# Two-layer graph convolution: 39 groups of three blocks by one-hot products and 30 blocks by gathered rows, in place of 38 and 33

## The chip, the cores and the metric

The kernel runs on one core of one Trainium2 chip, in one launch. The metric is the device time of that core in microseconds. Engine names are those of the profile: PE is TensorE's matmul stream and PEld its weight loads, DVE is VectorE, ACT is ScalarE, POOL is GpSimd, SP is SyncE, which here only issues DMAs.

## The reference, cut to what matters

```python
NTOKEN, NINP, NHID, NEDGE = 18750, 64, 128, 300000
def gcn_conv(x, W, b, src, dst, n):
    h = x @ W
    deg = jnp.zeros((n,), h.dtype).at[dst].add(1.0) + 1.0
    dinv = jax.lax.rsqrt(deg)
    norm = dinv[src] * dinv[dst]
    agg = jax.ops.segment_sum(h[src] * norm[:, None], dst, num_segments=n)
    return agg + h * (dinv * dinv)[:, None] + b
h = gcn_conv(emb, W1, b1, src, dst, NTOKEN)
nodes = gcn_conv(h, W2, b2, src, dst, NTOKEN)
return nodes[input.reshape(-1)].reshape(b_, l_, NINP)   # input: 512 x 200
```

The costly part is the sum over 300,000 edges into 18,750 nodes, done twice, once in each layer.

## The kernel before

The nodes are 147 blocks of 128 (`BLOCKS`). A node's row is 64 numbers held as three bf16 parts (`ROW` = 192 columns), and the table of all rows lies in SBUF (`xtab`) and in DRAM (`table`, for layer 1 `table1`).

**Before the layers** (to about 1075 us) the degrees are counted, the edges are sorted by a bitonic sort on DVE and PE, and the node rows are weighed. After it the sorted keys lie in DRAM and are read back by cell.

**Two ways of summing the edges of a destination block.** The destination blocks are split by the constant `SPE`:

- The first `SPE * SUP` blocks (38 groups of `SUP` = 3) are summed by one-hot products. A group has `CELLS` = 49 cells, one for every window of `WIN` = 3 source blocks. So there are `ST` = 49 * `SPE` cells, worked in batches of `BT` = 4: `NB` = 466 batches a layer. For a cell PE multiplies three one-hot matrices with three blocks of `xtab` (L989, "gather"), ACT copies the result to SBUF as `grow` (L830), and PE multiplies it by three one-hot matrices of the destinations (L1054, "scatter") into the group's sums. DVE makes both one-hots: `dwin` (L1560), one instruction for each cell, and `s_oh` (L1465), three instructions for each pair of batches. A batch therefore has 12 gather and 12 scatter matmuls of 192 columns.
- The other `ZB` = 33 blocks are summed by items "z": POOL gathers 128 rows from DRAM by one indirect DMA (L684) into one of `RING` = 18 places of `zring`, DVE makes one one-hot `zoh` (L1544), PE makes one matmul (L1020). A block has `ZT` = 18 such items, the last one 10. What did not fit into a cell goes the same way: `OT` = 3 * `SPE` items "o" (in layer 0, for its first groups, "m"), each with one gather, one one-hot `ooh` (L1547) and three matmuls (L1025; L1037 to L1043 for "m").

So a layer has 586 + 114 = 700 items. `planned` puts them into the batches by hand: each batch j is filled up to `total * (j + 1) // NB` items, o items go to the last three batches of their group, and the first item of a new z block waits until three batches after the last item of the block before:

```python
goal = total * (j + 1) // NB if j < NB - 4 else total
while left and given + len(now) < goal and (left[0][2] or j >= wait_until):
    ...
    if n == (ZT if blk < ZB - 1 else ZLAST) - 1:
        wait_until = j + 3
```

In layer 1 `wait_until` begins at 10. The order on PE is written out: in batch j it waits for DVE's `d_ready`, does the items of the batch, and then for each half the gather of batch j + 1 and the scatter of batch j, waiting for ACT's copy. DVE works one batch ahead and waits for `ymm` (the scatter of the batch before last); POOL waits for `zmm`, by which PE gives a place of the ring back. SP broadcasts the source numbers of two batches (`keys<-srel`, 256 KB) and stores finished groups. When a group closes, DVE takes its sums out (L1471), and when a z block closes, with L1477.

**After the layers** the requested rows are picked and written by indirect DMAs (L730, L739); that part has no `SPE` in it.

Of the kernel before, what the change touches and what calls it, by code (L numbers as in the profile page):

```python
# [52 lines left out]

SUP, SPE, WIN = 3, 38, 3
CELLS = BLOCKS // WIN
ST = SPE * CELLS
ZB0 = SPE * SUP
# [1658 lines left out]
```

## Time and profile before

| what | value |
|---|---|
| time, median of 3 runs | 4097.41 us (4090.86 to 4101.44) |
| time of the profiled execution | 4114.96 us |
| its span, first to last instruction | 4113.1 us |
| layer 0, layer 1 | 1357 us, 1288 us |
| PE, DVE, POOL busy over the span | 68%, 73%, 45% |
| mean granted TensorE clock | 0.848 |

Busy time is a share of the span; a granted clock of 1.0 is 2.4 GHz, 0.5 is 1.2 GHz. A matmul's duration in the trace covers its way through the array, and matmuls overlap; their pace is read from the starts. The wait named behind an idle time is the one that ended it; "remote" and "issue" are ends that the trace ties to no instruction.

### The profile page before, as it was taken

The page shows a single profiled execution, that of the slowest core. Times are in us where ns is not written, and L with a number is a line of the kernel's source. Part 1 is how long each engine was busy: PE and PEld are TensorE (multiplying, and loading weights), DVE is VectorE, ACT ScalarE, POOL GpSimd, SP SyncE. Part 2 cuts the span into 40 slices and gives each one's busy share as a digit, 9 for nine tenths or more (in the row PEclk, how much of TensorE's full clock was granted, in tenths as well). Part 3 has the DMA queues.
Part 4 walks back from the last instruction along what each step waited for, and adds up shares of the span by engine and source line. Part 5 has one row for each costly group of instructions (what it writes and reads, how often), then busy time and mean ns, then how long its engine had stood idle before and what let it go on. Part 6 is the DMA issues. An engine that isn't in the chain of part 4 may idle for free.

```text
span 4113.1 us, 74778 instructions
## 1 busy us (share of the span) xinstructions
PE 2787.5 (68%) x27730; PEld 2494.4 (61%) x27730; DVE 3019.4 (73%) x8656; ACT 1326.7 (32%) x3124; POOL 1867.6 (45%) x1717
## 2 busy tenths in 40 slices
PE   6996434421477888888888867888888888883000
PEld 5884222211367777877877766888887888882000
DVE  9999999999577887877777866777777777773000
ACT  5774212210433333433333322333333333331000
POOL 2000000000465556666656645666666565555765
PEclk9997566655699999999999988999999999996555
DMA  3000000000223233333333342333333333336400
GB/s 75 0 0 4 19 12 16 19 4 0 64 77 83 76 78 79 86 79 79 81 81 82 83 134 69 80 84 82 85 82 81 77 82 80 78 81 252 60 24 9
DMA packets 202648, 269.00 MB, mean 65 GB/s; under 512 B 99119, under 2 KB 111704, under 8 KB 202039
## 3 DMA queue, kind: packets, MB, share of 16 engines
q1 hardware_dynamic: 147912, 185.41, 15.1%
q0 software_dynamic: 54416, 79.31, 10.3%
q8 instruction: 203, 3.33, 0.3%
q14 instruction: 117, 0.96, 0.1%
HBM read 213.38 MB, written 52.14 MB: 65 GB/s over the span
## 4 chain that ended last, share of the span: by engine, by line
PE 47%; DVE 32%; issue 6%; another core or an unknown queue 6%; POOL 5%; ACT 2%; POOLq 1%; SPq 1%; DMA 0%; DVEq 0%; ACTq 0%
PE ps L989 17%; PE ps L1054 17%; PE ps L871 8%; DVE oh L1560 7%; DVE keys L1287 6%; DVE keys L1288 6%; DVE keys L1465 4%; POOL arena L730 3%; PE ps L1020 2%; POOL out L739 2%; DVE zoh L1544 2%; PE ps L937 1%; PE ps L1025 1%; POOLq L739 1%
## 5 line engine op out<-in xcount | busy, mean ns | idle before, releaser
L684 POOL DMA_INDIRECT zring<-table,sidx x1400 | 1560.2, 1114 | 1055.2 <-PE ps L1020 533.8
L989 PE MATMUL ps<-arena,keys 128*128 128x192 bf16 x11184 | 1283.9, 253 | 271.1 <-issue 132.1
L830 ACT ACTIVATE steps_oh<-ps 128x384 bf16<-128x384 f32 x1864 | 898.7, 490 | 1723.7 <-PE ps L989 1296.2
L1054 PE MATMUL ps<-steps_oh,oh 128*128 128x192 bf16 x11172 | 1276.9, 252 | 1.9 <-issue 1.9
L989 PEld LDWEIGHTS ps<-arena,keys 128*128 128x128 bf16 x11184 | 970.5, 100 | 340.1 <-issue 205.2
L1054 PEld LDWEIGHTS ps<-steps_oh,oh 128*128 128x128 bf16 x11172 | 985.7, 100 | 12.8 <-issue 3.1
L1560 DVE TENSOR_SCALAR oh<-io_h,dl 128x384 bf16<-128x384 int16 x3724 | 960.0, 319 | 44.9 <-remote 28.0
L1465 DVE TENSOR_SCALAR keys<-keys,lanes 128x1024 bf16<-128x1024 int16 x1398 | 596.5, 480 | 16.7 <-DMA keys<-srel 10.6
L639 POOL DMA_INDIRECT arena<-line,row_i x16 | 15.8, 988 | 1030.4 <-DVEq L1351 1025.9
L1544 DVE TENSOR_SCALAR zoh<-io_h,dl 128x128 bf16<-128x128 int16 x1172 | 261.2, 263 | 301.6 <-remote 147.5
L937 PE MATMUL ps<-ident,keys 128*128 128x128 f32 x464 | 100.1, 409 | 319.8 <-DVE keys L1288 315.3
L1020 PE MATMUL ps<-zring,zoh 128*128 128x192 bf16 x1172 | 217.7, 253 | 119.3 <-DVE oh L1560 79.7
L937 PEld LDWEIGHTS ps<-ident,keys 128*128 128x128 f32 x464 | 92.5, 222 | 335.6 <-DVE keys L1288 330.7
L1287 DVE TENSOR_TENSOR keys<-keys 128x1280 f32<-128x1280 f32 (+4 forms) x233 | 278.9, 1197 | 17.6 <-ACT keys L801 9.5
L1288 DVE TENSOR_TENSOR keys<-keys 128x1280 f32<-128x1280 f32 (+4 forms) x233 | 277.4, 1190 | 0.0
L758 ACT ACTIVATE steps_oh<-colf,arena 128x128 bf16<-128x128 f32 x784 | 240.4, 389 | 78.8 <-PE ps L871 78.7
L1138 DVE TENSOR_TENSOR oh<-iorep,arena 128x1024 bf16<-128x1024 bf16 (+1 forms) x392 | 258.6, 714 | 0.4 <-DVE arena L1188 0.4
L871 PE MATMUL ps<-oh 128*128 128x147 bf16 x1568 | 231.1, 314 | 0.3 <-DVE oh L1138 0.3
L1020 PEld LDWEIGHTS ps<-zring,zoh 128*128 128x128 bf16 x1172 | 99.2, 99 | 173.5 <-DVE oh L1560 119.2
L871 PEld LDWEIGHTS ps<-oh 128*128 128x128 bf16 x1568 | 173.2, 118 | 40.7 <-DVE oh L1138 17.6
L1547 DVE TENSOR_SCALAR ooh<-io_h,dl 128x384 bf16<-128x384 int16 x228 | 71.6, 324 | 161.2 <-PE ps L1054 89.6
L739 POOL DMA_INDIRECT out<-arena,oidx x130 | 127.7, 982 | 67.9 <-issue 67.9
(249 smaller groups left out, 1615.8 us busy)
## 6 DMA issues: line engine op xcount, KB each, us to landing
keys<-srel SPq DMA_DIRECT2D x466, 256.0 KB
out<-zring SPq DMA_DIRECT2D x1, 25600.0 KB
zring<-table,sidx POOLq DMA_INDIRECT x1400
table<-arena SPq DMA_DIRECT2D x19, 384.0 KB, 2.8
table<-sgn_l SPq DMA_DIRECT2D x38, 144.0 KB
nodes<-arena SPq DMA_DIRECT2D x38, 96.0 KB
arena<-in_L_rec_edge_index SPq DMA_DIRECT2D x2, 1171.5 KB, 6.6
arena<-nodes,oidx POOLq DMA_INDIRECT x130
```

Of the source, the lines that this page charges most:

```text
L684: pool.indirect_dma_start(out=zring[:, i % RING, :], out_offset=None, in_=rows_of, in_offset=bass.IndirectOffsetOnAxis(ap=sidx[:, col:col ...
L830: act.activation(grow[:, j % 2, h * 2 * ROW:(h + 1) * 2 * ROW], pg[h][:, 0:2 * ROW], ACT.Copy).then_inc(evac, 1)
L871: mm = pe.matmul(bank[:, 0:BLOCKS], lane[:, t // TT, :, t % TT] if steps is None else stp[:, t, :], blk[:, t // TT, :, t % TT], start=Fals ...
L989: mm = pe.matmul(pg[t // 2][:, t % 2 * ROW:(t % 2 + 1) * ROW], s_oh[:, j // 2 % 2, k, e:e + P], xtab[:, (w * WIN + k) * ROW:(w * WIN + k + ...
L1020: pe.matmul(pz[:, 0:ROW], zoh[:, u, :], zring[:, u, :], start=False, stop=(n == (ZT if blk < ZB - 1 else ZLAST) - 1)).then_inc(zmm, 1)
L1054: mm = pe.matmul(sums(sl, k), dwin[:, j % 2, t, k * P:(k + 1) * P], grow[:, j % 2, t * ROW:(t + 1) * ROW], start=False, stop=(w == CELLS - ...
L1138: dve.tensor_tensor(o.rearrange("p (s j t) -> p s j t", s=HH // TT, t=TT), iorep[:, 0:m, :].unsqueeze(1).to_broadcast([P, HH // TT, m, TT] ...
L1287: dve.tensor_tensor(b[:, :, 0, :], a[:, :, 0, :], a[:, :, 1, :], ALU.min).then_inc(k_stage, 1)
L1288: dve.tensor_tensor(b[:, :, 1, :], a[:, :, 0, :], a[:, :, 1, :], ALU.max).then_inc(k_stage, 1)
L1465: made = dve.tensor_scalar(s_oh[:, p % 2, k, :], srow[:, p % 2, :], lanes[:, k:k + 1], None, ALU.is_equal)
L1544: dve.tensor_scalar(zoh[:, place[item], :], io_h[:, 0:P], dl[:, col:col + 1], None, ALU.is_equal)
L1560: made = dve.tensor_scalar(dwin[:, j % 2, t, :], io_h[:, off:off + SUP * P], dl[:, c:c + 1], None, ALU.is_equal)
```

## The change

One constant:

```diff
-SUP, SPE, WIN = 3, 38, 3
+SUP, SPE, WIN = 3, 39, 3
 CELLS = BLOCKS // WIN
 ST = SPE * CELLS
 ZB0 = SPE * SUP
```

What follows from it by the kernel's own formulas, for each layer: `ST` 1862 becomes 1911, `NB` 466 becomes 478, `NPAIR` 233 becomes 239, `ZB` 33 becomes 30 (with `ZB0` 114 becoming 117), z items 586 become 532, `OT` 114 becomes 117, all items 700 become 649. `GT`, the number of cell tables of 128 cells, stays 15. `planned` spreads 649 items over 478 batches (1.36 a batch) where it spread 700 over 466 (1.50).

## Rows read from the trace of the kernel before

**Rows 1.** The page: span, engines, TensorE's clock in 40 slices.

```profile
span 4113.1 us, 74778 instructions
...
PE 2787.5 (68%) x27730; PEld 2494.4 (61%) x27730; DVE 3019.4 (73%) x8656; ACT 1326.7 (32%) x3124; POOL 1867.6 (45%) x1717
...
PEclk9997566655699999999999988999999999996555
```

**Rows 2.** Windows, both layers: length, busy PE, PEld, DVE, ACT, POOL, clock, DMA.

```profile
1075.00:2432.00 1357.00, 1117.86 (x12248) 1032.14 (x12246) 1045.33 (x3906) 490.36 (x1067) 813.02 (x725) 0.95 0.32 79
2448.00:3736.00 1288.00, 1104.05 (x12212) 1033.65 (x12210) 935.94 (x3505) 449.48 (x933) 763.69 (x692) 0.95 0.33 82
```

**Rows 3.** Timeline, PE, around a stop in layer 1 (start, us, idle before).

```profile
2982.14 0.66 PE L989 MATMUL ps<-arena,keys 128*128 128x192 bf16 x6
2982.63 0.66 PE L1054 MATMUL ps<-steps_oh,oh 128*128 128x192 bf16 x6
...
2984.57 0.66 PE L1054 MATMUL ps<-steps_oh,oh 128*128 128x192 bf16 x6
2988.26 1.14 PE L989 MATMUL ps<-arena,keys 128*128 128x192 bf16 x6 [3.03 <-issue]
```

**Rows 4.** The chain that ended last, both layers, by line.

```profile
by line: PE ps L989 26.0%; PE ps L1054 25.9%; DVE oh L1560 11.3%; another core or an unknown queue 8.7%; DVE keys L1465 5.4%; issue 5.0%; PE ps L1020 3.3%; DVE zoh L1544 3.3%; PE ps L1025 1.7%; ACT steps_oh L830 1.5%; DVE arena L1471 1.4%; 
```

**Rows 5.** Groups by line, both layers (busy us, mean ns, idle before, releasers).

```profile
L684 POOL DMA_INDIRECT zring<-table,sidx x1397 | 1557.1, 1115 | 1040.9 <-PE ps L1020 533.8 <-issue 287.6 <-remote 107.2
L989 PE MATMUL ps<-arena,keys 128*128 128x192 bf16 x11167 | 1281.0, 253 | 261.4 <-issue 132.1 <-ACT steps_oh L830 94.9 <-DMA arena<-table 17.7
...
L1560 DVE TENSOR_SCALAR oh<-io_h,dl 128x384 bf16<-128x384 int16 x3718 | 958.5, 319 | 44.9 <-remote 28.0 <-PE ps L1054 14.9 <-issue 1.1
...
L1544 DVE TENSOR_SCALAR zoh<-io_h,dl 128x128 bf16<-128x128 int16 x1169 | 260.6, 263 | 301.6 <-remote 147.5 <-PE ps L1054 146.5 <-issue 4.3
...
L1547 DVE TENSOR_SCALAR ooh<-io_h,dl 128x384 bf16<-128x384 int16 x228 | 71.6, 324 | 161.2 <-PE ps L1054 89.6 <-remote 66.9 <-issue 3.3
```

**Rows 6.** Timeline, POOL, the run of gathers after layer 1's first burst.

```profile
2489.35 0.94 POOL L684 DMA_INDIRECT zring<-table,sidx  x1 [0.30 <-issue]
...
2509.54 0.94 POOL L684 DMA_INDIRECT zring<-table,sidx  x1 [0.30 <-issue]
```

**Rows 7.** Timeline, PE, beside the run of rows 6.

```profile
2497.60 0.67 PE L1054 MATMUL ps<-steps_oh,oh 128*128 128x192 bf16 x6
2504.83 1.14 PE L989 MATMUL ps<-arena,keys 128*128 128x192 bf16 x6 [6.56 <-issue]
...
2517.01 1.12 PE L989 MATMUL ps<-arena,keys 128*128 128x192 bf16 x6 [10.07 <-ACT steps_oh L830]
```

**Rows 8.** Timeline, ACT, the stop of rows 3.

```profile
2987.71 0.87 ACT L830 ACTIVATE steps_oh<-ps 128x384 bf16<-128x384 f32 x2 [3.71 <-remote]
```

**Rows 9.** Timeline, POOL, before that stop of PE.

```profile
2979.26 0.94 POOL L684 DMA_INDIRECT zring<-table,sidx  x1 [0.30 <-PE ps L1020]
...
2985.65 0.94 POOL L684 DMA_INDIRECT zring<-table,sidx  x1 [0.30 <-issue]
```

**Rows 10.** Windows, one gathered block each, layer 1 (columns as in rows 2).

```profile
2671.10:2710.30 39.20, 36.61 (x421) 33.91 (x419) 32.52 (x123) 15.18 (x32) 24.89 (x23) 1.00 0.33 88
2749.10:2786.20 37.10, 33.10 (x369) 31.25 (x367) 27.67 (x105) 13.73 (x29) 23.55 (x21) 0.95 0.33 83
...
2824.10:2861.50 37.40, 32.09 (x372) 29.98 (x371) 28.45 (x106) 13.54 (x29) 24.30 (x22) 1.00 0.33 81
...
3446.70:3485.60 38.90, 33.13 (x368) 31.30 (x366) 28.07 (x106) 13.35 (x28) 22.45 (x21) 0.96 0.31 79
...
3525.70:3566.50 40.80, 34.76 (x373) 32.12 (x371) 28.90 (x108) 13.42 (x29) 23.18 (x22) 0.92 0.32 77
```

**Rows 11.** Windows, one gathered block each, layer 0.

```profile
1791.40:1831.20 39.80, 34.54 (x369) 31.71 (x367) 29.71 (x116) 14.41 (x33) 22.96 (x21) 0.91 0.32 84
...
2293.30:2335.50 42.20, 37.58 (x432) 34.74 (x432) 34.32 (x130) 15.98 (x35) 26.60 (x25) 1.00 0.41 91
```

## The prediction

> **What bounds the kernel now.** I read the page first: PE is busy 68% and DVE 73% of the 4113.1 us, no engine is full [rows 1], so the bound has to be sought by stage. The windows by stage give two layers of 1357 and 1288 us, 2645 us together; the change touches nothing else by any amount that matters. In them PE is busy 1117.86 + 1104.05 = 2221.9 us (84%), DVE 1981 us (75%), ACT 940 us, POOL 1577 us [rows 2]. At full clock six matmuls start every 0.49 us, 82 ns each [rows 3], so the 24 products of a batch take 1.98 us of PE, while a batch lasts 2645/932 = 2.84 us. The chain of waits agrees on the bound: L989 and L1054 hold 52% of it, DVE's two large one-hot lines 17%, the matmul and one-hot of z items 3.3% each, "o" matmuls 1.7% [rows 4]. So PE is the path, with DVE close behind.
>
> POOL comes after both, but not harmlessly. It waited 533.8 us for PE to give ring places back [rows 5]: gathers are ahead of their use, and a full ring of 18 places at 1.5 items a batch is twelve batches, some 30 us, of lead. But PE stops when POOL issues gathers back to back for long. After the first burst of layer 1 POOL issues a gather every 1.25 us from 2489.35 on, 17 in a row to 2509.54 [rows 6]; PE stops for 6.56 and then 10.07 us beside it, and runs on when POOL's run is over [rows 7]. In a normal block the same happens on a small scale: PE's last matmul of a half starts at 2984.57, the copy that its results should release starts only at 2987.71, "remote", and PE comes back at 2988.26 at the lower clock (L989's six spans take 1.14 us where they took 0.66) [rows 3, 8]; POOL had issued six gathers without a pause from 2979.26 to 2985.65 [rows 9]. What holds the releases back the trace does not say; that it goes with runs of gathers it does. Such a run follows each new z block: three batches without a z item fill the ring, then 4 or 5 items fall into one batch and free as many places at once. I cut the layers into windows of one z block. Where the planner has no burst (2671.1), 16 batches take 39.2 us, 2.45 each. Blocks of 14 batches with a burst of 4 take 37.1 and 37.4 us, with a burst of 5 38.9 and 40.8 us [rows 10]; at 2.45 to 2.46 they would take 34.4. So a 4-burst costs some 3 us and a 5-burst some 5. In layer 0 blocks without a full burst run at 42.2/16 = 2.64 and the 5-burst block costs 39.8 - 14 * 2.64 = 2.8 us over that [rows 11].
>
> **The change, part by part.** Two layers together.
>
> *Added: 24 batches.* Their price is that of a clean batch without its items. A clean batch is 2.46 us. It carries 1172/932 = 1.26 z items and 228/932 = 0.24 o items. A z item costs on the path something between 0.08 us (its matmul on PE [rows 3]) and 0.22 us (260.6/1169, its one-hot on DVE [rows 5]); the chain charges 6.6% of its 2661 us to 1172 items, 0.15 us, which I take. An o item lies between 0.20 (1.7% of 2661 over 228, chain) and 0.56 (with 0.31 us of DVE); I take 0.3. So 2.46 - 0.19 - 0.07 = 2.20 us, and 24 * 2.20 = **+52.8 us**. The floor is 1.98 each (47.5), the ceiling the mean with all stops, 2.84 - 0.26 = 2.58 (61.9).
>
> *Removed: 108 z items; added: 6 o items.* 108 * 0.15 = **-16.2 us** (8.6 to 24), 6 * 0.3 = **+1.8 us**. One group's closing reduces and three z blocks' closing reduces, and their store DMAs, cancel within a microsecond. The 108 gathers themselves take 1.25 us of POOL each, but are worth nothing as such: POOL has that lead. They count only through the bursts.
>
> *Moved: the bursts.* By `planned`, written out for both constants, layer 1 has 12 bursts of 4 and 11 of 5 after two empty batches; it will have 17 of 4 and 6 of 5. Layer 0 has 16 and 11, and will have 17 and 6. At 3.1 and 4.7 us, layer 1 goes from 88.9 to 80.9: **-8.0 us**. In layer 0 the DVE work of cell lists and late groups hides part; at half those prices, 1.6 and 2.4, 52.0 becomes 41.6: **-10.4 us** (none to -18 if full prices hold). The first burst of layer 1 falls from 15 items to 13, and two gathers less in its run are **-2.5 us**.
>
> *POOL less dense.* The items ask for 1.50 gathers in 2.46 us, and will ask for 1.36. With a gather each 1.25 us POOL is 76% taken and will be some 70%, so it catches up sooner: over a run of 6.25 us the demand falls by (0.61 - 0.56) * 6.25 = 0.3 gathers, 0.4 us, times 46 bursts at most -20. I take **-8 us**, since a run only counts where it is long enough to stop PE.
>
> *At nothing:* the sort, the weighing and the output rounds (no `SPE` in them); 54 fewer transposed columns before layer 0; the `keys<-srel` broadcasts, 6 more a layer, hidden as now by two batches of lead (if that cover went, L1465 on DVE would wait for each, and PE behind it). With 1.36 items the alternation of one and two items no longer keeps step with the `s_oh` work of every second batch; that could be 0.03 us a batch either way, +-10 us in the range only.
>
> Sum: 52.8 - 16.2 + 1.8 - 8.0 - 10.4 - 2.5 - 8 = **+9.5 us**. On the profiled execution's 4114.96 us this is 4124.5. That execution lies 17.6 us above the median of the runs, so I put the sum on the median: 4097.4 + 9.5 = **4107 us**.
>
> **A rule weighed.** An alternative reading of the stops is PE's own instruction stream: the trace marks PE's idle before L989 mostly as "issue", 132.1 of 261.4 us [rows 5]. The Trainium skill (Runtime: NRT & Kernel Launch, Instruction fetch mechanics) says that a sequencer fetches its next page while it runs the current one, in blocks of 256 instructions, and that crossing is "mostly hidden" in straight-line code. By that rule the stops are not fetches and the sum stays +9.5; were they fetches, they would come by instructions and not by bursts, which is the first rival below. The place of the stops, beside POOL's run, sides with the rule [rows 6, 7].
>
> **The rivals.**
>
> *A, the stops go with batches or instructions, not with z blocks.* Then each added batch brings the mean with its stops: 24 * 2.58 - 16.2 + 1.8 = +47.5, 4145 us. For it: "issue" before L989. Against it: the block without a burst, whose 16 batches show no lower clock (1.00) and 2.6 us of PE idle, against 4 to 6 us in shorter windows with a burst [rows 10]. Chance 0.20.
>
> *B, the other side: the sparser gathers no longer reach the length at which PE stops.* The run before the small stop has six gathers [rows 9], hardly more than PE stands. If the lower demand keeps a third of the 34 bursts of 4 below it, 11 * 2.4 = 26 us go, and the shorter runs elsewhere give their full double, 8 more: 9.5 - 26 - 8 = -25, 4072 us. It decides from about nine bursts gone clean. For it: bursts of 3 or fewer cost almost nothing. Against it: a burst of 4 over three idle batches is the same in both plans. Chance 0.20.
>
> *C, gathers set the pace.* Then 102 gathers less at 1.25 us are -127 us, and the time is 3970 us, the added batches being free. Against it: 533.8 us in which POOL waits for PE [rows 5]. Chance 0.02.
>
> My own case: 0.58.
>
> **How the numbers follow.** About 0.3% (12.3 us) is what a measurement of this kernel can tell from no change. My case spans -10 to +28 about +9.5 (item price 8.6 to 24 in place of 16, density 0 to -20, alternation +-10): of its 0.58 I put 0.19 over +12.3, 0.37 within, 0.02 under. A gives 0.19 slower and 0.01 same, B 0.17 faster and 0.03 same, C 0.02 faster. Together faster 0.21, same 0.41, slower 0.38. The range reaches from B's 4072 to A's 4145, rounded outward to 4070 and 4146.
>
> **What would show it.** Right: L989 and L1054 with 5736 and 5733 matmuls a layer; layers longer by some 2 to 8 us each; per-block windows near 2.42 us a batch where there is no burst; 4-bursts still 3 us. PE busy up by about 490 * 0.091 = 44 us (2221.9/24460 = 0.091 us a matmul) and its idle in the layers (423 us now) down by some 35. Wrong, towards A: PE's idle grows with the batches; towards B: POOL's runs stay short, PE's clock nears 1.00, idle falls by 60 or more. It would be wrong too if the stage before the layers or the output changed by more than 5 us.

## The result, and the profile after

| kernel, on the same chip | median | lowest to highest | runs |
|---|---|---|---|
| before | 4099.42 us | 4090.86 to 4111.49 | 4 |
| changed | 4042.61 us | 4029.36 to 4044.11 | 4 |

The changed kernel takes 0.9858 [0.9838, 0.9878] of the time before: 57 us less. The forecast was 4107, with a range from 4070 to 4146, so the result lies under the range. The profiled executions differ by 4114.96 - 4042.54 = 72.4 us, and the sums over the traces below go by them; some 15 us of these are that the profiled execution of the kernel before lies that much above its median. Of the four executions of the changed kernel in the fifth set of experiments two lie far above the others (4822 and 12513 us), and its time there is the middle of the other two.

The page of the changed kernel (span, busy times, clock in 40 slices), for [rows 1]:

```profile
span 4040.7 us, 75790 instructions
...
PE 2798.7 (69%) x28220; PEld 2525.0 (62%) x28220; DVE 3037.7 (75%) x8683; ACT 1354.8 (34%) x3170; POOL 1779.0 (44%) x1615
...
PEclk9997566655699999999999988999999999996555
```

The windows of both layers, for [rows 2], and below them the stages before and after the layers:

```profile
1075.00:2389.00 1314.00, 1122.46 (x12494) 1050.02 (x12492) 1055.75 (x3918) 503.52 (x1088) 762.01 (x675) 0.96 0.33 81
2404.00:3663.00 1259.00, 1112.85 (x12458) 1048.15 (x12456) 943.39 (x3518) 464.17 (x956) 726.46 (x641) 0.96 0.34 84
```

```profile
0.00:1075.00 1075.00, 562.80 (x3268) 426.27 (x3269) 1026.32 (x1213) 385.90 (x1123) 31.40 (x32) 0.73 0.06 17
3663.00:4040.70 377.70, 0.00 (x0) 0.00 (x0) 3.32 (x6) 0.42 (x1) 250.94 (x260) 0.50 0.32 90
```

All of the 72 us come out of the layers: 1357 became 1314 and 1288 became 1259. PE does more in them (2221.9 us became 2235.3) and idles less: 423 us became 2573 - 2235.3 = 337.7. The groups by line, for [rows 5]:

```profile
L684 POOL DMA_INDIRECT zring<-table,sidx x1296 | 1468.0, 1133 | 1049.3 <-PE ps L1020 595.2 <-issue 228.6 <-PE ps L1025 102.3
L989 PE MATMUL ps<-arena,keys 128*128 128x192 bf16 x11456 | 1304.5, 252 | 200.7 <-issue 107.7 <-ACT steps_oh L830 54.3 <-DVE oh L1560 19.3
...
L1560 DVE TENSOR_SCALAR oh<-io_h,dl 128x384 bf16<-128x384 int16 x3815 | 982.6, 319 | 35.7 <-remote 25.0 <-PE ps L1054 10.1 <-issue 0.4
...
L1544 DVE TENSOR_SCALAR zoh<-io_h,dl 128x128 bf16<-128x128 int16 x1062 | 246.8, 265 | 273.5 <-remote 132.9 <-PE ps L1054 129.7 <-issue 7.0
```

Before L989 PE idles 60.7 us less (261.4 to 200.7): 24.4 less "issue", 40.6 less waiting for ACT's copy. These are the two faces of the stop in [rows 3, 8]. POOL waits longer for PE than before (595.2 for 533.8), so gathers do not set the pace. In the chain by line, for [rows 4], "another core or an unknown queue", which is the "remote" of the timelines, falls from 8.7% to 6.0%:

```profile
by line: PE ps L1054 26.8%; PE ps L989 26.0%; DVE oh L1560 12.2%; DVE keys L1465 6.3%; another core or an unknown queue 6.0%; issue 4.9%; DVE zoh L1544 3.3%; PE ps L1020 3.2%; PE ps L1025 2.0%; DVE arena L1471 1.5%; ACT steps_oh L830 0.8%; 
```

The stop itself is still there. After layer 1's first burst POOL gathers without a pause (its timeline, for [rows 6]), and PE beside it stops for 2.89, 5.24 and 3.52 us (its timeline, for [rows 7], where two stops took 6.56 and 10.07):

```profile
2445.51 0.95 POOL L684 DMA_INDIRECT zring<-table,sidx  x1 [0.30 <-issue]
...
2466.35 0.95 POOL L684 DMA_INDIRECT zring<-table,sidx  x1 [0.30 <-issue]
2470.08 1.03 POOL L684 DMA_INDIRECT zring<-table,sidx  x1 [2.79 <-remote]
```

```profile
2456.09 1.14 PE L989 MATMUL ps<-arena,keys 128*128 128x192 bf16 x6 [2.89 <-issue]
...
2464.66 1.14 PE L989 MATMUL ps<-arena,keys 128*128 128x192 bf16 x6 [5.24 <-issue]
...
2470.28 1.14 PE L989 MATMUL ps<-arena,keys 128*128 128x192 bf16 x6 [3.52 <-ACT steps_oh L830]
```

### The profile page after: what moved, and what is told of

Same layout as the page of the kernel before. It is cut to its first block, busy times and chain, and to the rows that moved or that the text cites. A ratio compares the mean times of both kernels' runs of the same rounds, so it can differ in the third digit from the quotient of the medians.

```text
span 4040.7 us, 75790 instructions
## 1 busy us (share of the span) xinstructions
PE 2798.7 (69%) x28220; PEld 2525.0 (62%) x28220; DVE 3037.7 (75%) x8683; ACT 1354.8 (34%) x3170; POOL 1779.0 (44%) x1615
## 4 chain that ended last, share of the span: by engine, by line
PE 47%; DVE 34%; issue 6%; POOL 5%; another core or an unknown queue 4%; POOLq 1%; ACT 1%; SPq 1%; DMA 0%; DVEq 0%; ACTq 0%
PE ps L1054 17%; PE ps L989 17%; PE ps L871 8%; DVE oh L1560 8%; DVE keys L1287 7%; DVE keys L1288 6%; DVE keys L1465 4%; POOL arena L730 3%; POOL out L739 2%; DVE zoh L1544 2%; PE ps L1020 2%; PE ps L1025 1%; PE ps L937 1%; POOLq L739 1%
## 5 line engine op out<-in xcount | busy, mean ns | idle before, releaser
L684 POOL DMA_INDIRECT zring<-table,sidx x1298 | 1471.5, 1134 | 1063.1 <-PE ps L1020 595.2
L830 ACT ACTIVATE steps_oh<-ps 128x384 bf16<-128x384 f32 x1912 | 927.5, 491 | 1621.6 <-PE ps L989 1232.5
L989 PE MATMUL ps<-arena,keys 128*128 128x192 bf16 x11472 | 1307.2, 252 | 210.4 <-issue 107.7
L1054 PE MATMUL ps<-steps_oh,oh 128*128 128x192 bf16 x11466 | 1300.0, 250 | 0.0
L989 PEld LDWEIGHTS ps<-arena,keys 128*128 128x128 bf16 x11472 | 994.0, 100 | 264.5 <-issue 162.2
L1054 PEld LDWEIGHTS ps<-steps_oh,oh 128*128 128x128 bf16 x11466 | 1005.4, 100 | 9.9 <-issue 1.4
L1560 DVE TENSOR_SCALAR oh<-io_h,dl 128x384 bf16<-128x384 int16 x3822 | 984.3, 319 | 35.7 <-remote 25.0
L1465 DVE TENSOR_SCALAR keys<-keys,lanes 128x1024 bf16<-128x1024 int16 x1434 | 611.9, 481 | 12.3 <-DMA keys<-srel 6.4
L1544 DVE TENSOR_SCALAR zoh<-io_h,dl 128x128 bf16<-128x128 int16 x1064 | 247.3, 265 | 273.5 <-remote 132.9
L1020 PE MATMUL ps<-zring,zoh 128*128 128x192 bf16 x1064 | 208.0, 252 | 107.3 <-DVE oh L1560 60.1
```

Source lines behind the costliest of these rows:

```text
L684: pool.indirect_dma_start(out=zring[:, i % RING, :], out_offset=None, in_=rows_of, in_offset=bass.IndirectOffsetOnAxis(ap=sidx[:, col:col ...
L830: act.activation(grow[:, j % 2, h * 2 * ROW:(h + 1) * 2 * ROW], pg[h][:, 0:2 * ROW], ACT.Copy).then_inc(evac, 1)
L989: mm = pe.matmul(pg[t // 2][:, t % 2 * ROW:(t % 2 + 1) * ROW], s_oh[:, j // 2 % 2, k, e:e + P], xtab[:, (w * WIN + k) * ROW:(w * WIN + k + ...
L1020: pe.matmul(pz[:, 0:ROW], zoh[:, u, :], zring[:, u, :], start=False, stop=(n == (ZT if blk < ZB - 1 else ZLAST) - 1)).then_inc(zmm, 1)
L1054: mm = pe.matmul(sums(sl, k), dwin[:, j % 2, t, k * P:(k + 1) * P], grow[:, j % 2, t * ROW:(t + 1) * ROW], start=False, stop=(w == CELLS - ...
L1465: made = dve.tensor_scalar(s_oh[:, p % 2, k, :], srow[:, p % 2, :], lanes[:, k:k + 1], None, ALU.is_equal)
```

## The experiments

Eighteen kernels ran, in five sets (an expectation says "call" for a set). Each set ran on one chip, with its own runs of the kernel before, and the chips are of two kinds: on two of them (sets 1 and 2) the kernel before takes 3637 to 3638 us, on the others (sets 3 to 5), as on the recorded one, 4100 to 4145. Here they are "the quick chips" and "the recorded kind". Sets 3 and 4 bear the same chip's number, and yet the kernel before takes 1% longer in set 4; no chip was seen in both kinds. So each kernel is compared inside its own set.

### Set 1, a quick chip (before: 3638.21 us)

The planner's bursts, its alternation, and one group fewer:

```diff
 # e1_before_cap3 (on before) and e1_after_cap3 (on the changed kernel)
-while left and given + len(now) < goal and (left[0][2] or j >= wait_until):
+while left and given + len(now) < goal and (len(now) < 3 or j >= NB - 4) and (left[0][2] or j >= wait_until):
 # e1_before_phase (on before)
-goal = total * (j + 1) // NB if j < NB - 4 else total
+goal = (total * (j + 1) + NB // 2) // NB if j < NB - 4 else total
 # e1_spe37 (on before)
-SUP, SPE, WIN = 3, 38, 3
+SUP, SPE, WIN = 3, 37, 3
-FREE_FROM = 24
+FREE_FROM = 23
```

> The kernel before, but no batch gets more than 3 items, so that the 4- and 5-bursts after a z block's pause are spread over the next batches; batches, products, gathers and one-hots are the same in number. Theory R (PE stops with POOL's long runs of gathers, and the bursts make the runs): the 50 bursts stop costing, 60 to 120 us faster than before, 3980 to 4040 us, PE idle in the layers well under 423 us. Theory D (each item costs the path far more than the 0.15 us that I took, burst or not): within 15 us of before. Theory P (the time hangs on how the 1, 2, 1, 2 of items falls on the batches with source one-hots): within 15 us of before, either way.

> The changed kernel with the same limit of 3 items in a batch. Theory R: faster than the changed kernel by somewhat less than the limit gives before, 40 to 100 us, and the gap between the two capped kernels shrinks to under 20 us or turns round. Theory D: within 15 us of the changed kernel, and the gap of 57 us between 38 and 39 groups stays with the limit. Theory P: as D for this kernel.

> The kernel before with the planner's goal shifted by half an item, so that in the first half of a layer the batches with two items fall on the other parity (those with source one-hots), and back in the second half. Theory P: a change of more than 20 us. Theories R and D: within 12 us of before.

> 37 groups by one-hot products and 36 blocks by gathers (and one block more of scratch space given free early, since the scratch would not fit). Batches 454 a layer, items 751, 1.65 a batch. Theory D: the step of one group is again 40 to 75 us, now slower than before: 4140 to 4175 us. Theory R: three z blocks more a layer and a denser POOL, slower too, 20 to 60 us. Theory P: items a batch are out of step with the source one-hots as in the changed kernel, so it is at least 20 us faster than before. My recorded prediction's sum would give about 10 us faster than before.

| kernel | median | ratio to before |
|---|---|---|
| e1_before_cap3 | 3642.39 us | 1.0010 [1.0001, 1.0020] |
| e1_after_cap3 | 3661.34 us | 1.0066 [1.0049, 1.0083] |
| e1_before_phase | 3636.98 us | 1.0002 [0.9992, 1.0011] |
| e1_spe37 | 3706.95 us | 1.0202 [1.0185, 1.0219] |

At most 3 items a batch, and another phase of the alternation, change nothing that counts. But this chip could not say what bursts cost, because here PE hardly stops at all: on it the changed kernel with the limit is 23 us slower than before, not faster. With 37 groups (1502 gathers) 69 us are lost: POOL's gathers are busy 1693 of some 2280 us there, with 0.3 us more of issue each, so it is nearly full, and PE waits for gathered rows. Theory D had asked for 40 to 75 us, for another reason. So set 2 was to price the changed kernel's parts one by one, with work added that nobody reads; it met a quick chip again.

### Set 2, a quick chip (before: 3636.84 us)

e2_after is the changed kernel. The other three add unread work to it, one piece for every fourth item: 324 gathers, 324 one-hots, or 252 matmuls (only beside z items that are not the first of their block).

```diff
 # e2_gather4, in POOL's loop over the items of a layer
+if i % 4 == 3:
+    k = layer * (NI // 4) + i // 4
+    if k:
+        pool.wait_ge(extra_in, 16 * k)
+    pool.indirect_dma_start(
+        out=extra[:, :], out_offset=None, in_=rows_of,
+        in_offset=bass.IndirectOffsetOnAxis(ap=sidx[:, 0:1], axis=0)).then_inc(extra_in, 16)
 # e2_onehot4, on DVE
+dve.tensor_scalar(extra_oh[...], io_h[:, 0:P], dl[:, 0:1], None, ALU.is_equal)
 # e2_product4, on PE
+pe.matmul(pz[:, 256:256 + ROW], ident_h[:, :], xtab[:, 0:ROW], start=False, stop=False)
```

> The changed kernel itself, beside the kernel before on the chip of this call. The first four experiments ran on a chip on which the kernel before takes 3638 us, not 4099, and in their traces PE hardly stops inside POOL's runs of gathers. Theory R2 (the gain of 57 us lies wholly in those stops, and is no part of a chip without them): on such a chip the changed kernel is slower than before by 10 to 40 us; on a chip with the stops it is faster by 40 to 70. Theory D (an item costs the path much more than 0.15 us for a reason of the kernel's own): faster by 40 to 60 us on either chip.

> The changed kernel with one more gather by POOL after every fourth item, into a place that nobody reads: 324 gathers more, no work more on PE or DVE. Theory R2: on a chip without stops within 20 us of the changed kernel, as long as POOL keeps up (it is then at 812 gathers in a layer, some 1015 us of 1075), so up to 40 us if it doesn't; on a chip with stops over 150 us slower. Theory D, if the price of an item is its gather: over 150 us slower on both.

> The changed kernel with one more 128-column one-hot on DVE for every fourth item, 324 in all, read by nobody. R2 with the price of the recorded prediction: 324 * 0.07 to 0.22 us, 23 to 70 us slower. Theory D, if the price of an item is DVE's: over 150 us slower.

> The changed kernel with one more 192-column matmul on PE for nearly every fourth item (z items other than a block's first), some 230 to 260 in all, into columns that nobody reads. R2: 0.08 us each, 15 to 30 us slower. Theory D, if the price is PE's: over 100 us.

| kernel | median | ratio to before | over e2_after |
|---|---|---|---|
| e2_after | 3666.52 us | 1.0076 [1.0060, 1.0093] | |
| e2_gather4 | 3824.29 us | 1.0506 [1.0467, 1.0546] | +157.8 |
| e2_onehot4 | 3695.50 us | 1.0161 [1.0144, 1.0177] | +29.0 |
| e2_product4 | 3680.05 us | 1.0115 [1.0098, 1.0132] | +13.5 |

**The change makes the kernel slower on this chip, by 30 us.** It comes out of the layers, 2227 us where those of e1_before_phase, on the other quick chip, take 2195 (its time is that of the kernel before), and PE is busy 36 us longer in them. I read it as the price of the added batches less the items, near the 38.4 of the forecast; some relief of a nearly full POOL may be in it too. An item's one-hot costs 29.0/324 = 0.09 us and its matmul 13.5/252 = 0.05, together 0.14 where 0.15 was taken. What differs from the recorded kind is the stop. The windows of both layers of e2_after:

```profile
1075.00:2227.00 1152.00, 1065.92 (x12491) 1026.32 (x12489) 1054.10 (x3915) 508.54 (x1087) 772.04 (x674) 0.99 0.37 92
2245.00:3320.00 1075.00, 1047.39 (x12455) 1025.67 (x12452) 945.23 (x3518) 468.57 (x956) 748.66 (x641) 0.99 0.39 97
```

In layer 1 PE is busy 1047 of 1075 us at a clock of 0.99, where the changed kernel on the recorded kind has it busy 1113 of 1259 at 0.96. Yet POOL issues long runs here too, from 2286.76 to 2319.14 in the next timeline, and PE beside it (the second one) goes on every half microsecond:

```profile
2294.74 1.57 POOL L684 DMA_INDIRECT zring<-table,sidx  x1 [0.30 <-issue]
2296.61 3.57 POOL L684 DMA_INDIRECT zring<-table,sidx  x1 [0.30 <-PE ps L1020]
...
2319.14 0.94 POOL L684 DMA_INDIRECT zring<-table,sidx  x1 [0.30 <-issue]
```

```profile
2297.33 0.66 PE L989 MATMUL ps<-arena,keys 128*128 128x192 bf16 x6
2297.82 0.66 PE L1054 MATMUL ps<-steps_oh,oh 128*128 128x192 bf16 x6
2298.32 0.66 PE L989 MATMUL ps<-arena,keys 128*128 128x192 bf16 x6
```

e2_gather4 is limited by POOL itself: its two gather lines are busy 1456.9 + 354.3 us of 2400, plus 0.3 us of issue each, and PE now waits for gathered rows (the groups by line; on e2_after this line has 105.8 us of idle, 104.0 of it for DVE):

```profile
L1030 PEld LDWEIGHTS ps<-zring,zoh 128*128 128x128 bf16 x1063 | 95.8, 98 | 211.3 <-DVE oh L1570 121.6 <-DMA zring<-table,sidx 73.9 <-issue 12.7
```

So its 158 us, where at most 40 were expected without stops and over 150 by theory D, say what a full POOL costs, not what a gather costs in the kernel. Theory D itself had asked for a faster e2_after on this chip too.

### Set 3, the recorded kind (before: 4100.86 us)

Gathers alone, in both directions: 98 of 1400 left out from the kernel before, 98 of them added to the changed kernel (the probe above with 13 and 12 in place of 4 and 3), the limit of 3 again, and 40 groups. e3_before_fewer leaves out the 98 gathers only: their one-hots and matmuls stay and read what the ring holds, and PE does not wait for these 98 (in the kernel before no idle of PE in the layers ends with a gather's landing).

```diff
 # e3_before_fewer
+def left_out(i):
+    return i >= RING and i % 14 == 13
...
+                    if left_out(i):
+                        continue                      # POOL
...
+                    if not left_out(i):               # PE's wait for the gather
 # e3_spe40 (on before)
-SUP, SPE, WIN = 3, 38, 3
+SUP, SPE, WIN = 3, 40, 3
-LISTED, LIST_STEP, LATE_STEP = 150, 4, 25
+LISTED, LIST_STEP, LATE_STEP = 152, 4, 25
```

> The kernel before with every 14th gather of a layer left out, 98 of 1400 (their items use the rows that lie in their place of the ring, so the sums differ); batches, one-hots and products are those of before, only POOL and its DMAs have less to do, as in the changed kernel. Theory R2 (POOL's gathers stop PE, on chips that show the stops): on a chip on which the kernel before takes 4099 us, 60 to 100 us faster than before, since 57 of net gain and some 30 us for the added batches have to come from them. On a chip on which it takes 3638 us: within 15 us of before, up to 20 faster if POOL is at its limit there. A theory that puts the gain into fewer one-hots or matmuls: within 15 us on either.

> The changed kernel with one more gather by POOL after every 13th item, 98 in all, into a place nobody reads: it has the gathers of before (1396 of 1400) and the batches, one-hots and products of after. Theory R2: on a chip at 4099 us it loses the gain and 30 us more, 60 to 110 us over the changed kernel, 4100 to 4150; on a chip at 3638 us it is 0 to 20 us over the changed kernel's 3667. The other theory: within 15 us of the changed kernel on either.

> The kernel before with at most 3 items in a batch, as in the first call, for a chip with the stops. If the bursts of 4 and 5 make them, 60 to 120 us faster than before on a chip at 4099 us; if it is the number and density of gathers whatever their place, within 20 us of before. On a chip at 3638 us the first call gave 4 us over before, and the same is expected.

> 40 groups by one-hot products and 27 blocks by gathers, with the list stage two batches later since there is one cell table more. Theory R2: on a chip at 4099 us, where gathers are dear, again faster than the changed kernel by 20 to 60 us, some 4000; on a chip at 3638 us another 25 to 40 us slower, 3690 to 3705.

| kernel | gathers | median | ratio to before |
|---|---|---|---|
| e3_before_fewer | 1302 | 4033.52 us | 0.9838 [0.9809, 0.9867] |
| e3_after_gather13 | 1396 | 4153.88 us | 1.0133 [1.0099, 1.0167] |
| e3_before_cap3 | 1400 | 4105.85 us | 1.0019 [1.0005, 1.0033] |
| e3_spe40 | 1196 | 3976.79 us | 0.9696 [0.9670, 0.9721] |

Leaving 98 gathers out of the kernel before, with all matmuls and one-hots kept, gives 67 us, 0.69 each. Adding 98 to the changed kernel, which by the ratio takes 4100.86 * 0.9858 = 4042.6 us here, costs 111, 1.13 each. Spreading the bursts costs 5 us and gives nothing, where 60 to 120 us had been expected if the bursts make the stops. 40 groups take 66 us less than the changed kernel, where 20 to 60 had been expected. The kernel before has no trace of this set, and e3_before_cap3, whose time is within 0.2% of its, stands for it. The windows of both layers, first e3_before_cap3, then e3_before_fewer:

```profile
1075.00:2422.00 1347.00, 1121.55 (x12252) 1041.34 (x12250) 1047.21 (x3908) 490.52 (x1067) 817.45 (x725) 0.94 0.33 80
2438.00:3725.00 1287.00, 1114.71 (x12212) 1044.29 (x12209) 935.03 (x3505) 450.84 (x933) 764.60 (x692) 0.94 0.33 82
```

```profile
1075.00:2378.00 1303.00, 1101.46 (x12247) 1025.62 (x12245) 1042.71 (x3906) 490.90 (x1067) 759.48 (x676) 0.96 0.32 80
2394.00:3651.00 1257.00, 1096.21 (x12210) 1029.94 (x12208) 933.02 (x3505) 450.18 (x933) 727.94 (x643) 0.95 0.33 82
```

Same matmuls, same DVE work, 98 gathers apart: 74 us less in the layers. Half of it is PE's idle (2634 - 2236.3 = 397.7 becomes 2560 - 2197.7 = 362.3), the other half PE's busy time, since after fewer stops fewer matmuls run at the lower clock (0.94 in both layers, then 0.96 and 0.95).

### Set 4, the recorded kind (before: 4140.91 us)

What about a gather is it? All on the changed kernel, which by the ratio takes 4140.91 * 0.9858 = 4082 us here: 98 gathers of 32 bytes a row in place of 384; 98 iotas of 0.8 us on POOL; 94 plain loads of 48 KB from SP's queue.

```diff
 # e4_narrow13: the probe with
+            out=extra[:, 0:16], out_offset=None, in_=rows_of.rearrange("r (x e) -> (r x) e", e=16),
 # e4_compute13: in place of the gather
+        pool.iota(extra[:, :], pattern=[[1, 800]], base=0, channel_multiplier=0).then_inc(extra_in, 1)
 # e4_hw13: in SP's loop over pairs of batches, each fifth pair
+        sp.dma_start(extra[:, :], table[0:P, :]).then_inc(extra_in, 16)
```

> The changed kernel with 98 more gathers of 128 rows by POOL, as the run with 98 full gathers, but of 32 bytes a row in place of 384. If the rows and POOL's issuing of them hold PE up, the cost on a chip at 4099 us is near that of full gathers, 80 to 120 us over the changed kernel's 4043; if it is the bytes, under 30 us. On a chip at 3638 us under 20 us over 3667 by either.

> The changed kernel with 98 instructions of 0.8 us more on POOL that only write numbers into SBUF (iota, 128 x 800), no DMA. If it is GpSimd being busy that counts, 40 to 110 us over the changed kernel on a chip at 4099 us; if it is the gather as a DMA, under 15 us. On a chip at 3638 us under 15 us by either.

> The changed kernel with 94 loads more of 128 rows of 384 bytes on SP's queue, the bytes of a gather without GpSimd. If it is the DMA traffic or its completion that counts, 40 to 110 us over the changed kernel on a chip at 4099 us; if it has to be issued by GpSimd, under 15 us. On a chip at 3638 us under 15 us by either.

| kernel | median | ratio to before | over 4082 |
|---|---|---|---|
| e4_narrow13 | 4190.22 us | 1.0120 [1.0102, 1.0138] | +108 |
| e4_compute13 | 4124.40 us | 0.9963 [0.9945, 0.9980] | +42 |
| e4_hw13 | 4086.08 us | 0.9866 [0.9830, 0.9901] | +4 |

The bytes of a row do not matter, and loads from SP's queue cost nothing that can be told. The iotas cost 42 us, just inside what had been expected if a busy GpSimd counts by itself (40 to 110), yet well under the gathers' 108, so they ran again beside the changed kernel and the gathers.

### Set 5, the recorded kind (before: 4144.86 us)

The changed kernel, and the two probes on it again.

> The changed kernel, as the base of this call. On a chip where the kernel before takes 4099 to 4141 us, ratio 0.983 to 0.989 to before; on one at 3638 us, 1.006 to 1.010.

> 98 full gathers more on the changed kernel. On a chip at 4099 to 4141 us 90 to 125 us over the changed kernel of this call, as before. On a chip at 3638 us 0 to 20 us over it, if the price of a gather is a matter of the chip.

> 98 iotas more on POOL. On a chip at 4099 to 4141 us 30 to 55 us over the changed kernel of this call. On a chip at 3638 us under 15 us over it, if GpSimd's work holds PE up only on the other kind of chip; 30 us or more if it is DVE that it slows, on every chip.

| kernel | median | ratio to before | over 4084.5 |
|---|---|---|---|
| e5_after | 4084.5 us | | |
| e5_gather13 | 4194.01 us | 1.0133 [1.0101, 1.0164] | +109.5 |
| e5_compute13 | 4122.06 us | 0.9946 [0.9923, 0.9970] | +37.6 |

4084.5 is the middle of 4077.26 and 4091.75 and has no interval; 4144.86 * 0.9858 = 4086 agrees. The groups by line over both layers of e5_after, e5_gather13 and e5_compute13:

```profile
L989 PE MATMUL ps<-arena,keys 128*128 128x192 bf16 x11457 | 1308.9, 253 | 219.4 <-issue 121.6 <-ACT steps_oh L830 59.2 <-DVE oh L1560 19.9
...
L1560 DVE TENSOR_SCALAR oh<-io_h,dl 128x384 bf16<-128x384 int16 x3816 | 980.7, 318 | 39.8 <-PE ps L1054 34.7 <-remote 4.7
```

```profile
L999 PE MATMUL ps<-arena,keys 128*128 128x192 bf16 x11456 | 1311.1, 253 | 289.1 <-issue 169.6 <-ACT steps_oh L840 81.1 <-DMA arena<-table 19.2
...
L1570 DVE TENSOR_SCALAR oh<-io_h,dl 128x384 bf16<-128x384 int16 x3815 | 984.6, 319 | 33.8 <-PE ps L1064 26.5 <-remote 6.3 <-issue 0.7
...
L684 POOL DMA_INDIRECT extra<-table,sidx x98 | 104.3, 1064 | 29.9 <-issue 29.9
```

```profile
L997 PE MATMUL ps<-arena,keys 128*128 128x192 bf16 x11454 | 1303.7, 252 | 212.9 <-issue 103.9 <-ACT steps_oh L838 71.6 <-DMA arena<-table 18.3
...
L1568 DVE TENSOR_SCALAR oh<-io_h,dl 128x384 bf16<-128x384 int16 x3814 | 1043.4, 335 | 43.7 <-PE ps L1062 27.2 <-remote 16.1
...
L684 POOL IOTA extra<- 128x800 int32 x98 | 79.5, 812 | 0.8
```

The gathers leave DVE's one-hots at 319 ns and raise PE's idle before the same matmuls from 219.4 to 289.1 us, 48 us of it "issue" and 22 for ACT's copy. The iotas do not raise that idle (212.9); they lengthen DVE's large one-hots from 318 to 335 ns in the mean, 62.7 us over 3814. DVE's timeline beside the iota at 2595.79 shows how: four one-hots in 2.29 us where the next four take 1.05:

```profile
2595.11 2.29 DVE L1568 TENSOR_SCALAR oh<-io_h,dl 128x384 bf16<-128x384 int16 x4
...
2597.76 1.05 DVE L1568 TENSOR_SCALAR oh<-io_h,dl 128x384 bf16<-128x384 int16 x4
```

So two POOL instructions of similar length cost in different ways: beside an iota DVE is held up, beside a gather PE stops.

## Why the prediction was wrong, point by point

**The failed step is "POOL less dense", with the bursts beside it.** The sum had +38.4 for batches and items and -28.9 for all stops, -20.9 of it for the bursts and -8 for the density. On the quick chip, where PE hardly stops, the change measures +30, so the first term holds within 10 us. On the recorded kind it measures -57. If the first term is the same on both, the stops gave some -87 us, three times what I took, 0.85 us for each of the 102 gathers; that is an estimate over two chips, and the probes on the recorded kind alone give 0.69 and 1.13 from either side.

Where they went can be counted in the timelines of layer 1. A run is a row of gathers each starting within 1.62 us of the last (the row that fills the ring before the layer's first batch is left out); PE's idle beside it is taken up to 2.5 us behind its end:

| layer 1 | gathers | runs of 4 or 5: PE idle | runs of 6 or 7 | runs of 8 and more | all idle pieces over 0.15 us |
|---|---|---|---|---|---|
| before | 692 | 14: 19 us | 18: 62 us | 9: 56 us | 178 us |
| e3_before_cap3 | 691 | 13: 19 us | 16: 54 us | 11: 52 us | 167 us |
| e3_before_fewer | 642 | 13: 16 us | 21: 69 us | 3: 27 us | 156 us |
| changed | 640 | 12: 17 us | 16: 47 us | 6: 38 us | 140 us |
| e3_after_gather13 | 687 | 30: 44 us | 9: 28 us | 13: 77 us | 185 us |
| e3_spe40 | 586 | 13: 22 us | 14: 39 us | 1: 10 us | 103 us |
| e2_after (quick chip) | 640 | 15: 0 us | 20: 1 us | 27: 3 us | 24 us |

On the recorded kind a run of up to three costs some 0.2 us of PE, one of 4 or 5 about 1.4, one of 6 or 7 about 3.3, one of 8 or 9 about 5, and the layer's first, of 15 to 18 gathers, 10 to 16. Layer 0, counted in the same way, has a little over half of the gain: from before to changed its runs of 8 and more fall from 13 to 3, and its idle pieces from 234 to 186 us. That PE stops beside runs, as [rows 6, 7] had it, is right. Wrong was to tie the runs to the planner's bursts, which follow two batches without a z item, not the three that the prediction has in places. A limit of three items a batch leaves 27 runs of six or more, as many as before, and the same time: the ring's places come free 3 and 1 in place of 4 within a batch or two, and POOL still finds them all. The number of gathers over the stretch does change the long runs: 98 fewer over both layers leave three runs of 8 and more in layer 1, of nine in the kernel before and eleven in e3_before_cap3. That it does so by how far POOL is behind is argued, not shown. I had priced that as 0.3 gathers a burst and -8 us. The blocks of [rows 10] were read for what a burst costs, and a single block without a burst stood for the clean case. That their difference was the luck of a few long runs is argued.

**Rival A fell.** The Trainium skill (Runtime: NRT & Kernel Launch, Instruction fetch mechanics) has fetches mostly hidden, and the runs agree: e2_after has all 75,790 instructions of the changed kernel and idles 24 us in layer 1, and e3_before_fewer gains 67 us with PE's matmuls unchanged. The trace of before bears it out too: of PE's 51 stops of over 1 us in layer 1, four have one of the 98 transfers of 16 KB of the instruction queue (q8) within 1 us of them.

**Rival B had the mechanism and half of its size.** It said that a lower demand keeps runs below the length that stops PE, and gave -25 with 0.20. It took 34 us off my sum where 66 were needed, since it stopped at eleven bursts and one doubling. **Rival C came near the price (1.25 us a gather, for the 0.69 and 1.13 of the probes) for the wrong reason:** POOL does not set the pace, and waits for PE longer than before.

**Smaller steps.** PE busy was to rise by 44 us and rose by 13, since fewer matmuls ran at the lower clock: 2235.3/24952 = 0.0896 us each for 0.0908. Idle was to fall by 35 and fell by 85, beyond the 60 that was named as the sign of rival B. So the layers' 72 us are +44 for matmuls, -31 at the better clock, -85 of idle; the clock's part had no term of its own in my sum. L989 and L1054 have their 5736 and 5733 matmuls a layer but for a few missing records, and the stages around the layers stand still, as said. The alternation, put at +-10, is nothing (e1_before_phase, on a quick chip).

**A faster version.** By the same trade 40 groups take 0.9696 of the time before, 66 us under the changed kernel. Windows of both layers of e3_spe40, and PE's group:

```profile
1075.00:2354.00 1279.00, 1120.98 (x12736) 1054.45 (x12733) 1065.65 (x3940) 517.40 (x1115) 710.12 (x624) 0.97 0.33 82
2373.00:3597.00 1224.00, 1115.13 (x12699) 1059.80 (x12696) 954.45 (x3534) 475.57 (x981) 666.10 (x587) 0.97 0.33 85
```

```profile
L989 PE MATMUL ps<-arena,keys 128*128 128x192 bf16 x11742 | 1320.1, 250 | 164.2 <-issue 78.6 <-ACT steps_oh L830 48.7 <-DMA arena<-table 19.3
```

On the quick chips 38 groups are the best of 37, 38 and 39. The sign of this change went with the chip that it ran on: +30 us on one of the quick kind, -57 and -60 on two of the recorded kind.

**What stays open.** What in POOL's issuing of a gather holds back PE's and ACT's releases, the traces do not say; shown is that it goes with gathers issued by POOL, whatever their bytes, and not with loads from SP's queue. Why it is all but absent on the quick chips is open as well, and whether that is a trait of the chip or of what else ran beside it at the time: two chips of the one kind were seen and two or three of the other. The 98 gathers, the iotas and 40 groups were not tried there.

## What to carry to other kernels

Where an engine stops beside another's instructions for no reason that the trace names, price it by leaving some of those instructions out with all else kept: one such run gives the whole effect, where a few windows that look clean give only the part that you already suspect. A queue that is far ahead of its use, and waits for its consumers, can still cost a microsecond for each thing it issues. And look at a second chip before a constant is tuned on one.

## What the runs showed of the hardware

- The same kernel takes 3637 to 3638 us on two chips and 4100 to 4145 on the others, 4101 and 4141 in two sets with the same chip's number. On the first PE hardly stops beside gathers (24 us of idle in layer 1 of e2_after, for 140 in the changed kernel); the granted clock there is 0.99 for 0.96.
- On the second kind a gather of 128 rows issued by POOL costs 0.7 to 1.1 us of the kernel's time, though POOL has slack, and as much whether a row has 384 or 32 bytes (109.5 and 108 us for 98). A 48 KB load from SP's queue costs some 0.04 us (4/94, within the error).
- An iota on POOL holds up DVE: four one-hots took 2.29 us beside it for 1.05. The Trainium skill (SBUF — State Buffer, SBUF: two separate sides) has VectorE, in a two-port mode among others, and GpSimd share a pair of ports under an exclusive lock, by which the one that starts second blocks fully. That one is blocked the trace bears out: a single one-hot took 1.61 us, where their median is 0.31, and ended 0.11 us behind the iota of 0.81. But the trace has it starting 0.69 us before the iota, which is not the page's order, and no run here shows the mode of these one-hots.
